# A four-layer cross-attention kernel: TensorE turns the values back ahead of the second scores instead of behind the output product

## What is computed

```python
# every layer
q = heads(x @ Wq); k = heads(text @ Wk); v = heads(text @ Wv)
p = softmax(q @ k.T * scale)
x = merge(p @ v + branch(ip)) @ Wout + bout + x
# layer 3 alone: the branch over the 4 image tokens
qsem = l2norm(p @ text); sem = qsem @ l2norm(ip).T
branch = softmax(q @ k_ip.T * scale + 0.5 * sem) * spatial_mask @ v_ip
```

## Time and profile before

| what | value |
|---|---|
| median of 3 runs | 2361.54 us (2361.36 to 2363.28) |
| the profiled execution: its own time | 2364.91 us |
| the profiled execution: span from first to last instruction | 2363.1 us |
| mean granted clock of TensorE in the span | 0.968 |
| TensorE matmuls busy | 2177.9 us, 92% |
| VectorE busy | 1397.6 us, 59% |
| ScalarE busy | 1076.6 us, 46% |
| GpSimd busy | 459.0 us, 19% |

### The profile page before, as it was taken

One profiled execution on the slowest core, in us unless ns is written; L12 is line 12 of the kernel. 1 busy time (PEld: TensorE's weight loads), 2 busy tenths in 40 slices (PEclk: granted clock), 3 DMA queues, 4 the chain that ended last, 5 costly groups with the idle time before them and its releaser, 6 DMA issues. The chain is left out here.

```text
span 2363.1 us, 74795 instructions
## 1 busy us (share of the span) xinstructions
PE 2177.9 (92%) x26394; PEld 1807.6 (76%) x26394; DVE 1397.6 (59%) x4195; ACT 1076.6 (46%) x2733; POOL 459.0 (19%) x870
## 2 busy tenths in 40 slices
PE   1699999999999999999999999999999999999976
PEld 1578787788788778878878887887878778888765
DVE  3236666566566566656656665665666566566554
ACT  0244444445445444544544454454455445444431
POOL 0012212221121211221212121122122112221210
PEclk9799999999999999999999999999999999999985
DMA  2111111111111111111111111111111111111000
GB/s 85 49 46 37 51 48 36 46 48 44 37 50 43 37 50 49 39 42 49 44 37 50 45 39 46 50 42 40 49 44 37 50 43 42 45 50 35 24 10 5
DMA packets 92280, 101.21 MB, mean 43 GB/s; under 512 B 37313, under 2 KB 68505, under 8 KB 91898
## 3 DMA queue, kind: packets, MB, share of 16 engines
q1 hardware_dynamic: 90220, 92.86, 14.1%
q10 hardware_dynamic: 1678, 3.33, 0.5%
HBM read 34.13 MB, written 5.41 MB: 17 GB/s over the span
## 5 line engine op out<-in xcount | busy, mean ns | idle before, releaser
L1056 DVE TENSOR_REDUCE top<-ps_s 128x6 f32<-128x462 f32 (+3 forms) x1024 | 514.7, 547 | 186.9 <-PE ps_s L687 184.2
L954 ACT ACTIVATE p_t<-ps_s 116x512 f32<-116x512 f32 (+1 forms) x768 | 370.3, 544 | 68.8 <-PE ps_s L714 68.5
L1096 DVE TENSOR_TENSOR weighted<-ps_k,probs 128x462 f32<-128x462 f32 (+1 forms) x256 | 143.2, 559 | 328.7 <-PE ps_k L784 325.2
L687 PE MATMUL ps_s<-k_blocks,q_sb 32*128 32x231 f32 (+1 forms) x3584 | 296.5, 377 | 16.0 <-issue 15.9
L759 PE MATMUL ps_c<-p_t,v_rows 116*27 116x128 f32 (+1 forms) x7168 | 285.0, 282 | 14.2 <-DMA v_rows<-v_img 11.7
L1272 POOL TENSOR_TENSOR k_blocks<-k_sb,mask_k 128x231 f32<-128x231 f32 x384 | 211.6, 572 | 426.5 <-PE ps_s L714 411.5
L759 PEld LDWEIGHTS ps_c<-p_t,v_rows 116*27 116x27 f32 (+1 forms) x7168 | 212.1, 108 | 84.9 <-issue 49.1
L827 PE MATMUL ps_c<-o_t,wo 128*80 128x128 f32 x2048 | 275.4, 278 | 0.5 <-ACT o_t L982 0.5
L982 ACT ACTIVATE o_t<-ps_c 80x256 f32<-80x256 f32 x256 | 97.0, 379 | 336.9 <-PE ps_c L815 238.8
L714 PE MATMUL ps_s<-q_sb,k_blocks 32*116 32x128 f32 (+1 forms) x5376 | 229.2, 286 | 20.3 <-DMA q_sb<-top_t 11.4
L687 PEld LDWEIGHTS ps_s<-k_blocks,q_sb 32*128 32x128 f32 x3584 | 198.0, 185 | 57.9 <-issue 40.7
(11 more groups left out here) (112 smaller groups left out, 2904.6 us busy)
## 6 DMA issues: line engine op xcount, KB each, us to landing
v_rows<-v_img SPq DMA_DIRECT2D x128, 227.4 KB
context<-in_ctx SPq DMA_DIRECT2D x64, 336.0 KB, 3.0
q_sb<-top_t SPq DMA_DIRECT2D x576, 6.0 KB
v_rows<-v_img SPq DMA_DIRECT2D x64, 115.2 KB
v_rows<-v_img SPq DMA_DIRECT2D x64, 112.2 KB
x_in<-in_x SPq DMA_DIRECT2D x64, 80.0 KB, 1.8
out_x<-x_out SPq DMA_DIRECT2D x64, 80.0 KB, 1.7
v_rep<-v_dram SPq DMA_DIRECT2D x64, 50.0 KB
```

Of the source, the lines that this page charges most:

```text
L687: ins = pe.matmul(ps_s[:, z * 512 + j * GT:z * 512 + j * GT + n], q_sb[c % 3][lo:lo + QUAD, j * S:(j + 1) * S], k_blocks[c % 3][lo:lo + QU ...
L954: act.activation(to, source, ACT.Exp, scale=SCALE).then_inc(p_ready, 1)
L1056: dve.tensor_reduce(top[c % 2][:, z * BH:z * BH + m], s.rearrange("p (h t) -> p h t", t=T)[:, :, 0:n], AX.X, ALU.max).then_inc(s_top, 1)
L1096: dve.tensor_tensor(weighted[:, lo * T:hi * T], ps_k[:, 0:(hi - lo) * T], probs[:, lo * T:hi * T], ALU.mult).then_inc(w_ready, 1)
```

## The change

On TensorE alone, `turn_back` of unit `t-2` moves from behind the output product to a place ahead of `second`. No instruction is added or removed, and no other engine's order changes.

```diff
                 if topped(t):
                     turn_top(k, t)
+                if exists(t - 2):
+                    turn_back(k, t - 2)
                 if exists(t - 1):
                     second(k, t - 1)
                 if e_waves(t):
                     gram_wave(k, t, 1)
                 if layer(t) != L - 1 and out(t):
                     project_out(k, t)
-                if exists(t - 2):
-                    turn_back(k, t - 2)
                 if e_keys(t):
                     keys(k, t)
```

## The result

| | before | changed |
|---|---|---|
| median of 4 runs each, us | 2361.45 (2360.59 to 2363.28) | 2418.28 (2415.33 to 2420.07) |
| ratio | | 1.0238 [1.0221, 1.0256] |
| profiled execution, its own time, us | 2364.91 | 2418.88 |
| span, us | 2363.1 | 2417.1 |
| mean granted clock of TensorE | 0.968 | 0.975 |

What follows compares the result with a forecast made beforehand. The prediction took TensorE's queue to set the time (matmuls busy 92% of the span). Its terms, 28.8 + 10.8 + 13.9 + 8.3 = 61.8 us, added to 2361.5 gave 2423 us, forecast range 2401 to 2443, stated overall as 2398 to 2443.

Steps and rivals of the forecast that it cites:

- Term 1: `t % 4 == 0` step: the moved transposes wait for ScalarE's copy to `u_sb`, 0.45 us in 64 cycles, 28.8 us.
- Term 2: `t % 4 == 0` step: later output product delays VectorE's chain to the maxima, so `turn_top` waits longer, 10.8 us.
- the sign that the prediction gave: In the changed kernel's profile, L815 would be idle by 0.1 to 0.3 us for `o_sb`.
- Term 3: `t % 4 == 1` step: VectorE's chain to `o_last` moves by 0.22 us, lost in TensorE's wait for it, 13.9 us.
- Term 4: `t % 4 == 3` step: later second scores make ScalarE end later, holding the next step's scores 0.15 us, 8.3 us.
- `t % 4 == 2`: In this step the output product comes 0.22 us later, but nothing waits for it: no cost.
- (a): Rival: faster, as `o_sb` comes sooner in the `t % 4 == 3` step; down to 2297 us, chance 3%.
- (b): Rival: no change, the new wait is swallowed by TensorE's later waits of 0.26 and 0.76; 2361.5 us, chance 4%.
- (c): Rival: only the new `u_sb` wait and little else, as unseen slack eats the other terms; 2390 to 2401 us, 9%.
- (d): Rival: the new gap makes TensorE's clock fall; 2532 us if every cycle, 2459 in a third, chance 5%.

Runs made afterwards that it cites:

- e3: The changed kernel, but in the `t % 4 == 0` steps the transposes stand behind the sixth of the 14 transposes L731, still ahead of the output product: 2390.28 us.
- e5: The changed kernel, with ScalarE copying the product twice in the `t % 4 == 0` steps, first into a tile nobody reads: 2443.9 us.
- e9: The kernel before, with the transposes ahead of the second scores only in the `t % 4 == 3` steps: 2364.91 us, a single execution.
- e7: The kernel before, with the transposes ahead of the second scores only from step 255 on: 2361.14 us against 2362.92 before.
- e6: The changed kernel, with scores and queries ahead of what needs `o_last` in the `t % 4 == 2` steps: 2363.17 us against 2362.92 before.
- e1: The changed kernel, but in the `t % 4 == 0` steps the transposes stay behind the output product: 2383.35 us, ratio 1.0084.

## Why the prediction was right, and where it was off

The direction, the size and the mechanism held: 2418.28 us against 2423, within the range. By its own steps:

- **Term 1, the new wait, 0.45 us in each cycle.** Right, and slightly too small. The pair starts 0.05 us after the copy's end as taken from the earlier trace rows (1232.12 + 0.38 = 1232.50, start of the weight load 1232.55). The pair itself takes 0.27 us there and not 0.22, so that the step loses 0.51: 32.6 us over 64 cycles instead of 28.8, well inside the bounds. e3, where the wait is covered, gives 28.0 us back; e5, where it is longer by 0.27, loses 0.27 per cycle.
- **Term 2, 0.22 in 49 cycles.** Right. L745 still waits (46 times), and `turn_top` is 0.22 later against the scores. It holds in the plain cycles and is missing in the ten longer ones, where L745 waits in neither kernel; this is what the 45 of 59 in the earlier trace rows had said. By these figures it is between 10.8 and 12 us. Of the sign that the prediction gave, L815 idle by 0.1 to 0.3, the starts show 0.16; on the matmul rows it has 1.6 us in 9 times.
- **Term 3, 0.22 in 63 cycles, 13.9 us.** This is the term that was mis-sized. It is 0.10 in the plain cycles and 0.22 in the ten longer ones, some 7.5 us if the cycles behind the branch count as plain, and outside the bounds of 11 to 14. The shift of the pair is 0.22, but where `turn_top` came late the scores behind it lose 0.11 of their own time, once they don't directly follow it. The prediction took the duration of L714 for fixed. The earlier trace rows show it at 1.14 us; the row of this very step, 1.25, was not among its rows.
- **Term 4, 0.15 in 55 cycles, 8.3 us.** Right: the starts show 0.15, e9 alone 0.14.
- **`t % 4 == 2`: nothing.** Right. L714 is 0.22 later there and L603 not at all.
- **The last part.** Not in the prediction: -4.3 us in the profiled runs. The sum treated all 64 cycles alike. Behind the last unit the scores that cover `turn_out` are missing, and the clock is at the lower level for half of the time, 14.6 us less of it in the changed kernel's trace. e7, the test of it, shows no gain in its median.

The measured terms give 0.51 + 0.22 + 0.10 + 0.15 = 0.98 per plain cycle; the forecast was 61.8 / 64 = 0.97. So the near hit in the steady part is in part luck: term 1 was too small by 3.8 us and term 3 too large by some 6. What is left of the difference, 61.8 against 56.8, is about what the profiled runs show in the last part.

The rivals. (a), faster: `o_sb` came 1 us sooner in `t % 4 == 3`, VectorE's reciprocal no longer waited, and nothing in the steady part hung on it, as argued. (b), swallowed by the later waits: these grew (L800 44.0 to 48.0 us, L745 12.4 to 13.7), and e6 shows that the loss doesn't hang on L800's wait. (c), only term 1: e1 shows 0.25 per cycle without it. (d), the clock falls: the granted clock between 154 and 2200 us is 0.99 in both kernels, and between the first and the 59th L800 it is lowered in no cycle but those behind the branch, in either trace. Of the changed kernel (us, busy times of the engines, then the clock):

```profile
154.00:2200.00 2046.00, 1946.38 (x23731) 1594.74 (x23726) 1227.63 (x3665) 983.31 (x2457) 409.65 (x768) 0.99 0.16 43
```

The Trainium skill ("TensorE: Matmul & The Clock Gate", section "A second HAM failure mode: psum-queue depth-cycling") tells of short idle times between groups of matmuls that made the clock swing in another kernel. In this trace they did not: with a further wait of 0.47 us in each cycle it stays at 0.99.

Open are how the last part's 4.3 us divide, the 8 us or so by which e5 exceeds its cycles, and the spread of the cycles behind the loop's branch. All three go with time at the lower clock, which no experiment held fixed.

## What to carry to other kernels

An instruction that reads another engine's copy of a product needs other work between it and the product for as long as the copy takes to arrive; here 0.45 us of that had no cover, and moving the instruction forward past its cover cost it once per cycle although the instruction is only 0.2 us long. An instruction moved ahead on a full queue delays everything that it passes: ask which of these start chains on another engine, since such a chain can lose it for good while the queue gets it back. Here the chains of three steps lost some of it, and that of `t % 4 == 2` nothing. And where the queue stands still for one result, look for work behind it that doesn't need this result: putting the scores ahead of the wait for `o_last` gained 60 us, about as much as the change lost. Last, before a shorter stretch is put down to the order of work, look at its granted clock.

## What was not expected of the hardware

- The duration of a group depends on what stands ahead of it. In the `t % 4 == 1` step the second scores take 1.25 us directly behind a late `turn_top` and 1.14 behind two transposes, and the keys take 1.16 behind the pair and 1.26 without it. In the `t % 4 == 2` step the keys take 1.21 with and without it, so the pair alone isn't the reason. The pair costs 0.22 in the midst of L731 (e3) and 0.27 behind its own wait. In these cases some 0.05 to 0.1 us appear where TensorE has just waited or the first operand is just ready. That it is the first weight load, no longer hidden behind the matmul ahead, fits these rows but was not tested.
- A wait of 0.47 us stands at 0.28 us on the matmul rows, because the modelled end of the matmul ahead covers part of it. The weight-load rows and the starts show the whole.
- Two copies on ScalarE, 0.38 us each, start 0.28 us apart.
